# A two-layer max-aggregation graph network with expert-choice experts on one core: tile order by mixed ranks, joined first pairs, and the layer 2 table split on VectorE instead of sent through memory

## The reference, cut to what matters

```python
# x: 1250 x 512 f32; 41250 edges (src, dst) sorted by dst, self loops among them
def _graph_conv_max(x, src, dst, W_rel, b, W_root):
    agg = jax.ops.segment_max(x[src], dst, num_segments=N)
    return agg @ W_rel.T + b + x @ W_root.T
h = relu(_graph_conv_max(layernorm(x), ..., W1_rel, b1, W1_root))   # layer 1
h = relu(_graph_conv_max(h,            ..., W2_rel, b2, W2_root))   # layer 2
x = x + h
# experts: 8, each takes the 512 rows with the largest router weight of layernorm(x)
x = x + ffn(layernorm(x))          # gelu(sel @ W1 + b1) @ W2 + b2, weighted, added back
```

## Time and profile before

| what | before |
|---|---|
| median of 3 runs (lowest, highest) | 1026.27 us (1025.17, 1026.45) |
| the profiled execution's own time | 1024.63 us |
| its span, first to last instruction | 1022.6 us |
| mean granted clock of PE | 0.886 |
| busy: PE, DVE, POOL, ACT | 716.0, 719.3, 572.0, 236.2 us |
| until the first tile of layer 1 starts on DVE | 142.7 us |
| layer 1, to the end of its last merge | 431.5 us |
| layer 2, to the end of its last merge | 796.8 us |

### The profile page before, as it was taken

The page is one execution under the profiler, slowest core; times in us unless marked ns, Lnnn a source line. Parts: engine busy times, 40 slices in busy tenths (PEclk is TensorE's granted clock), DMA queues, the critical chain, the costliest instruction groups (busy, mean ns, idle before and its releaser), DMA issues.

```text
span 1022.6 us, 9802 instructions
## 1 busy us (share of the span) xinstructions
PE 716.0 (70%) x2593; PEld 322.9 (32%) x2593; DVE 719.3 (70%) x1313; ACT 236.2 (23%) x281; POOL 572.0 (56%) x561
## 2 busy tenths in 40 slices
PE   0329248999998889345887878776874512999997
PEld 0224013333333333112333333332331311444442
DVE  3769838888999988514899999989998596331110
ACT  0275231233333333002012222112200100122222
POOL 5650476566777777765445555666566203445533
PEclk9759669999999999657999999988987755999999
DMA  5740576566666766679556666666664702556746
GB/s 136 221 116 2 165 208 200 162 182 187 192 202 191 206 190 212 215 252 245 148 177 200 178 186 192 204 207 186 183 196 151 276 0 76 93 120 104 131 55 81
DMA packets 66460, 169.54 MB, mean 166 GB/s; under 512 B 16633, under 2 KB 21029, under 8 KB 66400
## 3 DMA queue, kind: packets, MB, share of 16 engines
q0 software_dynamic: 42240, 130.79, 47.0%
q1 hardware_dynamic: 16887, 18.45, 6.4%
q10 hardware_dynamic: 7288, 19.76, 5.7%
HBM read 145.72 MB, written 23.11 MB: 165 GB/s over the span
## 4 chain that ended last, share of the span: by engine, by line
DVE 31%; PE 30%; issue 16%; DMA 10%; POOL 7%; DVEq 2%; ACT 2%; POOLq 0%; SPq 0%; ACTq 0%
PE pp L1097 8%; PE pp L1417 6%; DVE weights L906 6%; PE pp L1404 5%; DVE acc L895 5%; DMA mem<-tab,ic 5%; POOL mem L838 4%; PE prow L1068 3%; DMA weights<-hotd 2%; PE prow L1037 2%; PE prow L1056 2%; DVE acc L975 2%; DVE mem L1274 2%; DVE mem L608 1%; DVE weights L908 1%
## 5 line engine op out<-in xcount | busy, mean ns | idle before, releaser
L838 POOL DMA_INDIRECT mem<-tab,ic x372 | 391.9, 1054 | 230.3 <-issue 100.3
L1097 PE MATMUL pp<-weights,slots 128*128 128x512 bf16 x1200 | 303.9, 403 | 136.2 <-DVE acc L895 85.0
L895 DVE TENSOR_TENSOR acc<-acc,pp 128x1024 f32<-128x1024 f32 x180 | 219.0, 1217 | 31.8 <-PE pp L1097 25.5
L906 DVE TENSOR_TENSOR weights<-weights,mem 128x1024 f32<-128x1024 f32 x166 | 203.3, 1225 | 25.3 <-SPq L805 14.2
L1097 PEld LDWEIGHTS pp<-weights,slots 128*128 128x128 bf16 x1200 | 117.2, 102 | 321.2 <-DVE acc L895 100.1
L1068 PE MATMUL prow<-weights,aggT 128*128 128x512 f32 x160 | 84.1, 654 | 13.7 <-ACT aggT L1162 13.7
L1385 DVE COPY weights<-prow 128x512 f32<-128x512 f32 x32 | 20.8, 687 | 98.7 <-PE prow L1037 98.1
L1456 POOL DMA_INDIRECT out<-mem,node_of x32 | 50.3, 1571 | 67.6 <-ACT mem L1434 58.8
L1056 PE MATMUL prow<-weights,rootT 128*128 128x512 f32 x160 | 74.2, 606 | 0.0
L1417 PE MATMUL pp<-weights,mem 128*128 128x512 f32 x128 | 63.5, 618 | 0.0
L908 DVE SCALAR_TENSOR_TENSOR weights<-carry,cap,mem 128x1024 f32<-128x1024 f32 x20 | 25.7, 1284 | 48.7 <-SPq L805 39.7
(11 more groups left out here) (361 smaller groups left out, 792.0 us busy)
## 6 DMA issues: line engine op xcount, KB each, us to landing
slots<-ttd ACTq DMA_DIRECT2D x20, 640.0 KB, 5.7
mem<-tab,ic POOLq DMA_INDIRECT x372, 3.8
weights<-in_L_ffn_W SPq DMA_DIRECT2D x9, 512.0 KB, 9.6
weights<-in_L_ffn_W ACTq DMA_DIRECT2D x7, 512.0 KB, 4.1
xnd<-xin ACTq DMA_DIRECT2D x10, 256.0 KB, 3.2
mem<-in_x SPq DMA_DIRECT2D x2, 1120.0 KB
tab<-mem SPq DMA_DIRECT2D x1, 2240.0 KB
weights<-in_L_gnn_W_rel SPq DMA_DIRECT2D x2, 1024.0 KB, 12.4
```

The lines of the kernel that those rows point to most:

```text
L838: g.indirect_dma_start(ring[:, h * PAIR + k, :], None, tables[l], bass.IndirectOffsetOnAxis(ic[:, j * PAIR + k:j * PAIR + k + 1], 0))\
L895: v.tensor_tensor(acc[:, :, :], acc[:, :, :], pp[j % 2][:, :, :], ALU.max).then_inc(S["pa"], 1)
L906: v.tensor_tensor(accg, accg, pair, ALU.max).then_inc(S["done"], 1)
L1097: ins = t.matmul(pp[j % 2][:, i, :], sel[u][:, j * KP + i, :], hot[:, j, w, :], start=w == 0, stop=w == 2)
```

## The change

**Mixed ranks.** The records of tiles 1 to 9 are read in three strided DMAs: tiles 1 to 3 get what were tiles 3, 6, 9, tiles 4 to 6 what were 2, 5, 8, and tiles 7 to 9 what were 1, 4, 7. The heaviest tile is now tile 3 (`HEAVY`), and `cap` and `carry` serve it alone.

**Joined first pairs.** `first_three` takes the place of four DVE instructions at the start of a tile by two: `acc` is the maximum of gathered pair 0 and table pair 0, and `accg` that of gathered pairs 1 and 2. Tile 3 and tile 13 need three. Tile 0 does all its table pairs first, then the gathered ones, the first two joined.

**No `hotd`.** `clamp`, `split_a`, `split_b`, ACT's three parts and the ten scatters of `hotd` are gone. In tile 10 SP loads `tab2` in node order into `stage` (f32, six groups of one or two chunks, twelve DMAs). For each chunk DVE writes the high part and the remainder (`high`, two instructions), ACT the middle part (`middles`), DVE the low part (`lowest`), and PE's table pair waits for it. The merge of layer 2 loses one instruction of 512 columns.

**Order around the layers.** POOL fetches own and input rows while DVE still builds the lists, and SP holds the write of `tab1` back until the ten `runs` have landed. `root` of tile 10 moves ahead of the last neighbour product of layer 1, and its root product to the front of tile 10.

```diff
-HPARTS = ((0, 2), (2, 5), (5, NC))
+HPARTS = ((0, 1), (1, 2), (2, 4), (4, 6), (6, 8), (8, NC))
+HEAVY = 3
...
-        s.dma_start(recs[:, 1:NQ, :], recd[LIGHT:N, :].rearrange("(q p) c -> p q c", p=P)).then_inc(S["recs"], 16)
+        ranked = recd[LIGHT:N, :].rearrange("(q p) c -> p q c", p=P)
+        for i, first in enumerate((2, 1, 0)):
+            s.dma_start(recs[:, 1 + 3 * i:4 + 3 * i, :], ranked[:, first:NQ - 1:3, :]).then_inc(S["recs"], 16)
...
+        for q in range(NQ):
+            s.wait_ge(s_run[q], 16)
         for lo, hi in PARTS:
             s.dma_start(tab1[0:N, :].rearrange("(c p) d -> p c d", p=CN)[lo:hi], big_x[lo:hi, :, :])\
...
+        after(g, cv, n_nodei)
+        input_rows(range(HQ, NQ))
+        g.wait_ge(S["tab"], n_tab)
+        first_rows(range(HQ, NQ))
+        after(g, ca, n_low[NC - 1])
+        first_rows(range(0, HQ))
+        input_rows(range(0, HQ))
...
             if l:
-                s.wait_ge(S["sch"], 16 * NQ)
-                s.wait_ge(S["pairs"], NQ * PAIRS)
                 for i, (c0, c1) in enumerate(HPARTS):
                     for lo, hi in PARTS:
-                        s.dma_start(hot[lo:hi, c0:c1, :, :].rearrange("p c w d -> p c (w d)"), hotc[lo:hi, c0:c1, :])\
-                            .then_inc(s_hx[i], 16)
+                        s.dma_start(stage[lo:hi, c0:c1, :], tabc[lo:hi, c0:c1, :]).then_inc(s_hx[i], 16)
...
-                    g.wait_ge(S["hl"], q + 1)
-                    g.indirect_dma_start(hotd, bass.IndirectOffsetOnAxis(nodeo[:, q:q + 1], 0), split_row[q], None)\
-                        .then_inc(S["sch"], 16)
...
+            def first_three(k, lo):
+
+                v.wait_ge(S["ready"], first_pair + lo + (FLYING + 1))
+                v.wait_ge(S["pairs"], k * PAIRS + 1)
+                v.tensor_tensor(acc[:, :, :], in_ring(lo), pp[0][:, :, :], ALU.max).then_inc(S["pa"], 1)
+                v.wait_ge(S["pa"], k * PAIRS + 1)
...
+                    v.wait_ge(S["ready"], first_pair + lo + (FLYING + 3))
+                    v.wait_ge(S["done"], first_pair + lo + SUBS)
+                    v.tensor_tensor(accg, in_ring(lo + 1), in_ring(lo + 2), ALU.max).then_inc(S["done"], 3)
+
+            def high(c):
+
+                v.wait_ge(s_hx[HGROUP[c]], 32)
+                v.tensor_scalar(hot[0:CN, c, 0, :], stage[0:CN, c, :], TOP, None, ALU.min).then_inc(S["hh"], 1)
+                v.wait_ge(S["hh"], c + 1)
+                v.scalar_tensor_tensor(stage[0:CN, c, :], stage[0:CN, c, :], TOP, hot[0:CN, c, 0, :], ALU.min, ALU.subtract)\
+                    .then_inc(S["hr"], 1)
+
+            def lowest(c):
+
+                v.wait_ge(S["hm"], c + 1)
+                v.tensor_tensor(hot[0:CN, c, 2, :], stage[0:CN, c, :], hot[0:CN, c, 1, :], ALU.subtract).then_inc(S["hl"], 1)
...
-                    if k == NQ and j in HSTARTS:
-                        t.wait_ge(s_hx[HSTARTS[j]], 32)
+                    if k == NQ:
+                        t.wait_ge(S["hl"], j + 1)
```

More of the change, by code:

```diff
@@ L256, in build @@
         s_run = [sem(f"s_run{q}") for q in range(NQ)]
-        s_hx = [sem(f"s_hx{i}") for i in range(3)]
+        s_hx = [sem(f"s_hx{i}") for i in range(len(HPARTS))]
         s_w1 = [sem(f"s_w1_{e}") for e in range(NX)]
@@ L905, in pool_pair @@
[L905 to L916 removed]
+                v.tensor_tensor(accg, accg, in_ring(slot), ALU.max).then_inc(S["done"], 1)
@@ L1125, in pe_tile @@
                 pairs(k, (3, 4))
-                root(k)
+                if k != NQ:
+                    root(k)
                 pairs(k, (5,))
-                root_product(k, range(C))
-                if l == 0 and q:
-                    split_a(q - 1)
-                pairs(k, (6, 7))
-                if l == 0 and q:
-                    split_b(q - 1)
-                pairs(k, (8, 9))
+                if k != NQ:
+                    root_product(k, range(C))
+                pairs(k, (6, 7, 8, 9))
                 if l and q:
```

222 lines of the change are left out of this document (120 added, 102 removed).

## The result

The median of four runs is **1009.77 us** (1008.24 to 1011.58), against 1026.22 for the kernel before beside it: ratio 0.984, 95% interval 0.982 to 0.986. The change is faster by 16.5 us. The forecast was 989, 37 faster: the sign is right and the time lies just inside the upper end of the range (970 to 1010), but more than half of the gain is missing. The profiled execution took 1008.71, its span is 1006.9, and the mean granted clock is 0.876.

The account below looks back on a forecast made before the run. PE's order or DVE bounds layer 1's tiles, gathers its heaviest; DVE bounds layer 2. Terms -23.5 + 4.6 - 15.4 - 3 = -37.3 against 1024.6 give 987.3; the median lies 1.6 above: 989, range 970 to 1010.

Parts of the forecast that it names:

- the term between the layers and tile 10: From the merge of tile 9 to that of tile 10: 71.5 us in place of 66.9, +4.6 (-2.4 to +8.6).
- The first chunk, 14.5: Start of tile 10: first table chunk lands 14.5 us after tile 9's merge, with neighbour products at 3.7, not 6.6.
- the last term: Behind layer 2: a last tile of 11 pairs keeps PE's clock, products take 3.7 instead of 6.6: -3 (0 to -3).
- 9.7 ahead of the steps: Tile 10, from first chunk to the eight steps: 9.7 us at the cold end, 8.3 at the warm end.
- The steps: Tile 10: DVE and PE wait for each other in eight steps, each 5.9 us at 1.2 GHz or 4.7 at 2.4.
- the warm end: Rival, tile 10: PE keeps 2.4 GHz, 50 us in place of 57, total 982; chance 0.20.
- Tile 0: Start: earlier gathers and table pairs first end tile 0 at 155 us with the preparation, against 167.4.
- the preparation: Before tile 0: the write of `tab1` moves behind `runs`, for -1.5 us (0 to -2).
- Tiles 1 to 9: Layer 1: the join mostly returns as a wait, lighter PE gives 25.0 at 8 pairs; 253 us, ending at 408.
- The rival in which gathers set layer 1: Layer 1: gathers at 3.1 us a pair end it at 424, 16 later; total 1005, chance 0.13.
- most indirect DMAs become the long kind: Rival, layer 1: joins slow POOL's gathers to 3.5 us a pair, layer 1 ends at 461; total 1042, chance 0.07.
- Tiles 11 to 19: Layer 2: join 1.1 a tile, merge 0.43 less, heavy tile loses 1.4 of gather waits: -15.4 us.

Follow-up runs that it names:

- e11: The change plus earlier split, moved gathered pair, late table transfers (978.63 us together), with unread PE matmuls added in tile 9: 976.92 us.
- e5: The change with nine unread PE matmuls ahead of each table pair from the third on in tile 10: 1004.72 us.
- e10: The change with tile 0 in the joined order of the other layer 1 tiles, a gathered pair first: 1020.21 us.
- e7: The change with POOL's twenty row fetches put back behind the lists, as in the kernel before: 1011.81 us.
- e4: The change with one gathered pair in layer 1 moved from the loop to between table pairs 2 and 3: 1001.29 us.
- e2: The change with the join of the first pairs undone in tiles 1 to 9 and 11 to 19: 1018.64 us.
- e3: The change with the ranks in rising order again, tile 9 the heaviest, records read by one strided DMA: 1011.30 us.

## Why the prediction was right or wrong

**The failed step is the term between the layers and tile 10**: "14.5 + 57 = 71.5: +4.6 (-2.4 to +8.6)" stood there, and 81.6, +14.7, came, above the term's own upper bound. Of the 10.1 us too much, the first chunk has 2.4, what lies ahead of the steps 6.6, and the steps 1.1:

- *The first chunk, 14.5.* It was 16.9. The forecast had "PE warm in a last tile of 11 pairs" and the products at 3.7; they took 5.82. The number of pairs was the wrong thing to go by: PE stood still for 4.1 us in the loop of tile 9 and for 3.1 before the merge. Ahead of the second pause four transposes took 0.60, and four of the same size behind it 1.11, so the clock fell in that pause. e11 filled both pauses and got 3.70, and the first chunk came at 14.4. The same error is in the last term: behind layer 2 the products took 5.40, not 3.7, and the gain was 1.8, not 3.
- *9.7 ahead of the steps.* From the first chunk (430.14) to the first step (446.44) it took 16.3. The prediction asked when the chunks would be there and never whether the gathers would: they were asked for at the same time as 2.5 MB of table and took 7.9 us to land. Waits of 5.9 for gathers and 1.85 for chunk 2 are the missing 6.6 and more. The row that should have warned was in the chain of the earlier trace rows: a bulk transfer of 25 us from 454.4 on, at this very place. In the kernel before, POOL asked for the first gathers of tile 10 at 453.3, beside it, and DVE took the first of them at 464.3:

```profile
464.34 1.28 DVE L908 SCALAR_TENSOR_TENSOR weights<-carry,cap,mem 128x1024 f32<-128x1024 f32 x1 [19.25 <-SPq L805]
```

This is the largest single miss, and no rival named it. The prediction's own sign for it, tile 10 over 65 us from its first chunk, was missed by a little: it took 64.7.

- *The steps.* 5.9 and 4.7 were given for the low and the high clock; the terms listed for them add up to 5.77 and 4.51, and 5.79 (the change) and 4.45 (e5) were measured. That mechanism, with its two prices, was right. 57 left 43.2 for the eight steps, and they came to 44.3: five of 5.79, two of 5.37 and 5.25 in which the clock rose for a part, and a last one of 4.73, since no chunk was left for `high`. That 43.2 lay so near is in part luck: it was a value between 37.6 and 47.2, and neither the clock's rises nor the short last step was in it.

The sentence cited from the Trainium skill ("TensorE: Matmul & The Clock Gate", Part 1), that the ramp costs under 1% of a typical kernel's span, is not contradicted by this case: the 7.5 us of e5's tile 10 are 0.7% of 1009. But it prices the rise of the clock at a kernel's beginning and says nothing of a loop like this one, so it was no reason to expect the warm end. Six of the eight table pairs ran at 2.72, and 0.7% is nearly half of what the whole change gained.

**Tile 0** (forecast 155, measured 156.9). Both of its reasons hold, and e10 and e7 show that the order is the larger. The gathers began at 133.4, not 131: with the fetches beside them the slots came later (e7), and PE began its table pairs no earlier than before (126.3 for 125.8 in the earlier trace rows), so the 1.5 us taken for the preparation did not come through.

**Tiles 1 to 9** (forecast 253, measured 256.4). "2.1 of the 2.3 us come back as a wait" was right, and e4 and e2 are its proof: the wait was 2.2 in most tiles, and without the join layer 1 is no longer. The heavy tile was 36.4 long, where the sum had 33.4 + 3, and 1.1 for `carry` and 2 for the low clock beside them, so nothing is missing there. Two tiles of 8 pairs came out longer than 25.0 by 2.9 and 1.5, with 2.7 and 3.3 us of waits for gathers. One follows tile 0, the other the heavy tile. The prediction had counted gather waits inside the heavy tile alone. The rival in which gathers set layer 1 went too far: waits for gathers of 2 us and more stand in four of its ten tiles (1, 3, 4 and 7). Nor did most indirect DMAs become the long kind: over the 372 gathers their mean went from 1.05 to 1.03 us.

**Tiles 11 to 19** (forecast -15.4, measured -10.4). The join was sized at 1.1 a tile and e2 measured 0.96. The heavy tile was to gain 2.9 and gained 0.2 (41.1 for 41.3). DVE's busy time fell to 34.0 from 35.3, but its last table pair ahead of the loop waited for PE and came 12.2 us after the merge before, as in the kernel before (12.1): the join paid nothing, as e2 shows too. The 1.4 us of gather waits that a full ring was to save stayed as well: in the loop they were 2.6 before and 2.7 now. That is 2.7 of the 5.0 missing. A tile of 9 pairs (the ninth of layer 2) took 32.0 with a wait of 2.2 for PE, where the other such tile took 30.1; why, no run tried.

**The mixing** had no term of its own but was behind "starts with a full ring", and e3 shows 1.5 us, which cannot be told from nothing.

## What to carry to other kernels

When work moves from a transfer into a tile, write the order of both engines out as one cycle and ask whether each waits for the other in turn. If so, look one item further ahead before pricing the instructions: here the order cost 20 us of waits where the new instructions themselves took 18. When a bulk load is put next to the first small gathers of a phase, price the gathers' landing by a stretch with such a load in it, not by a quiet one. A pause of PE is not free even where nothing waits for it: look for the next thing on the path that PE does after it.
